# Local attention's sixteen steps written out, the second layer's weights brought in early, and two smaller moves at the head of a transformer kernel

## What is computed

```python
# block 1: 16-head causal attention, scores of masked keys set to 0 (not -inf), 64 wide heads
# block 2: mixture of 16 experts, top 2 of a softmax: y = x + sum_k w_k * (gelu(x @ W1[e_k] + b1) @ W2[e_k] + b2)
# block 3: counter = softplus(sum(relu(normed @ normed.T)) @ W1 + b1); concat([x, counter]) @ W2
# block 4: two layers of local attention, 8 heads, window 64
for l in range(2):
    h = shift_token(x)
    q, k, v = split(h @ wqkv[l])
    q = l2norm(q) * q_scale[l];  k = l2norm(k) * k_scale[l]
    q, k = rotary_xpos(q, k)                 # the same tables of cos, sin and scale for both layers
    x = x + local_attention(q, k, v) @ wo[l]
    h = layernorm(shift_token(x)) * ln_g[l] + ln_b[l]
    a, g = split(h @ w1[l] + b1[l])
    x = x + (a * gelu(g)) @ w2[l] + b2[l]
```

## Time and profile before

| | |
|---|---|
| time, 3 runs | 943.25 us median, 940.85 to 944.63 |
| profiled execution | 942.32 us; its span, first to last instruction, 940.5 us |
| busy PE, DVE, ACT, POOL | 786.5, 661.7, 590.3, 527.4 us |
| start, until the slots' staging begins | 0 to 19.3 us |
| block 1, 64 slots | to about 283 us |
| block 2, routing and experts | to about 440 us |
| block 3 | to about 496 us |
| block 4, local attention | to the end |

### The profile page before, as it was taken

One profiled execution on the slowest core, in us unless ns is written; L12 is line 12 of the kernel. 1 busy time (PEld: TensorE's weight loads), 2 busy tenths in 40 slices (PEclk: granted clock), 3 DMA queues, 4 the chain that ended last, 5 costly groups with the idle time before them and its releaser, 6 DMA issues. The chain is left out here.

```text
span 940.5 us, 21922 instructions
## 1 busy us (share of the span) xinstructions
PE 786.5 (84%) x6366; PEld 583.6 (62%) x6366; DVE 661.7 (70%) x1986; ACT 590.3 (63%) x1784; POOL 527.4 (56%) x603
## 2 busy tenths in 40 slices
PE   4899999999989844982554789999899999998884
PEld 3677777777769734981441356666666666666563
DVE  4777777777776765553675577888688888887555
ACT  2678888888860002761441568888788888886560
POOL 3644444444452773336834867777677777775411
PEclk9999999999999855995896899999999999999898
DMA  7544444444410081431100000000100000000001
GB/s 179 178 178 151 151 151 151 151 152 150 153 48 2 32 265 58 114 102 47 43 12 12 1 1 2 1 2 2 34 11 0 26 7 0 0 2 2 12 1 35
DMA packets 60796, 61.58 MB, mean 65 GB/s; under 512 B 13515, under 2 KB 48830, under 8 KB 60606
## 3 DMA queue, kind: packets, MB, share of 16 engines
q1 hardware_dynamic: 58686, 56.63, 18.4%
q0 software_dynamic: 2048, 4.20, 1.5%
HBM read 17.55 MB, written 23.00 MB: 43 GB/s over the span
## 5 line engine op out<-in xcount | busy, mean ns | idle before, releaser
L666 POOL TENSOR_TENSOR scratch<-scratch 128x256 f32<-128x256 f32 (+1 forms) x128 | 105.8, 827 | 132.6 <-DVE scratch L1644 132.6
L1043 ACT ACTIVATE scratch<-psum,scratch 128x128 f32<-128x128 f32 x256 | 113.9, 458 | 48.0 <-DVE scratch L1991 46.2
L794 POOL TENSOR_TENSOR big<-big 128x512 f32<-128x512 f32 x64 | 81.2, 1269 | 71.8 <-DVE big L1972 71.8
L898 ACT ACTIVATE scratch<-psum,scratch 128x256 f32<-128x256 f32 x256 | 118.0, 480 | 4.0 <-DVE scratch L1662 3.2
L803 POOL TENSOR_TENSOR scratch<-scratch,mhalf 128x16 f32<-128x16 f32 x32 | 93.0, 2906 | 16.8 <-DVE scratch L1978 16.8
L1415 PE MATMUL psum<-wqkv,scratch 128*128 128x512 f32 x128 | 71.2, 644 | 8.0 <-SPq L570 3.7
L1963 DVE TENSOR_REDUCE scratch<-big 128x8 f32<-128x512 f32 x64 | 43.7, 683 | 45.3 <-ACT big L1017 45.1
L1148 PE MATMUL psum<-scratch 128*128 128x256 f32 x240 | 61.8, 380 | 0.0
L1655 DVE TENSOR_TENSOR psum<-psum,causal 128x512 f32<-128x512 f32 x64 | 44.8, 700 | 23.0 <-PE psum L1171 22.9
L1989 DVE TENSOR_REDUCE scratch<-psum 128x4 f32<-128x512 f32 x64 | 44.0, 687 | 21.8 <-PE psum L1473 20.7
L1171 PE MATMUL psum<-scratch 64*128 64x128 f32 (+1 forms) x512 | 59.3, 350 | 0.0
(11 more groups left out here) (278 smaller groups left out, 2206.6 us busy)
## 6 DMA issues: line engine op xcount, KB each, us to landing
routed_in<-zfill SPq DMA_DIRECT2D x64, 256.0 KB, 2.2
scratch<-w_qkv SPq DMA_DIRECT2D x60, 193.0 KB, 2.2
scratch<-xT SPq DMA_DIRECT2D x60, 128.0 KB, 2.1
scratch<-routed_in SPq DMA_DIRECT2D x47, 64.0 KB, 1.8
routed_out<-scratch SPq DMA_DIRECT2D x23, 128.0 KB, 1.8
big<-in_L_ffn_W SPq DMA_DIRECT2D x1, 2048.0 KB, 8.9
wqkv<-in_L_ffn_wqkv SPq DMA_DIRECT2D x2, 512.0 KB
big<-in_L_ffn_b SPq DMA_DIRECT2D x1, 1024.0 KB, 11.8
```

The costliest lines, as they stand in the source:

```text
L666: pool.tensor_tensor(y, y, rs[s][:, t, :].unsqueeze(2).to_broadcast([P, 2, n]), ALU.mult).then_inc(b_p, 1)
L794: pool.tensor_tensor(qk[s][t][:, j * INNER:(j + 1) * INNER], t1[i % 2], t2[i % 2], ALU.add).then_inc(f_add, 1)
L898: last = act.activation(pr[s][:, t, h, :], scores_of(s)[:, h, t * S:(t + 1) * S], ACT.Exp, bias=nb[s][:, 2 * t + h:2 * t + h + 1], accum_o ...
L1043: last = act.activation(p1[k][:, h, t, :], bank(h)[:, t * P:(t + 1) * P], ACT.Exp, bias=nb1[k][:, h, t:t + 1], scale=rq8[s][:, t, 2 * a + ...
```

## The change

- Local attention's steps -3 to 17 are all written out; `run_steps` has no loop.
- The second layer's weights go to tiles of their own, cut from `w_qkv0` and `w_o0`, which are free after block 1's output projection. SyncE loads them (seven DMAs, 1.5 MB) right behind the experts' weights, and waits for their landing there, ahead of its wait for the routing. The five semaphores are raised for all 16 units at once.
- `lv` and `rotc` are gone: the engines read `vec` and `rot` at the layer's place. The two copies before step 0 and the loads during steps 6 to 10 are gone, with SyncE's waits for them.
- VectorE's slot begins with `z_out(g - 1)` and `inverse_sums(g + 1, 1 - s, 0)`, where the slot before ended with `z_out(g)` and `inverse_sums(g + 2, s, 0)`: VectorE's instructions keep their order, and the border between two passes of the loop falls elsewhere.
- x is loaded in four DMAs of 256 KB with a semaphore each, and VectorE's statistics wait for one chunk at a time.
- GpSimd raises `const_ready` after the first constants, and puts the four powers between the making of the others.

```diff
-            full = (4, UNITS - 4)
-            for n in range(-3, full[0]):
+            for n in range(-3, UNITS + 2):
                 step(n, n % 2)
-            with eng.Fori(0, (full[1] - full[0]) // 2) as i:
-                for s in range(2):
-                    step(i * 2 + (full[0] + s), s)
-            for n in range(full[1], UNITS + 2):
-                step(n, n % 2)
-                if after:
-                    after(n - full[1])
+                if after and n >= UNITS - 4:
+                    after(n - UNITS + 4)
...
+        spare = w_qkv0[:, :, :].rearrange("p a n -> p (a n)")
+        wqkv1s = (wqkv1[:, :], spare[:, 0:3 * INNER])
+        wo1s = (wo1[:, :, :], spare[:, 3 * INNER:3 * INNER + PAIRS1 * D].rearrange("p (a d) -> p a d", d=D))
+        wf1s = (wf1[:, :], spare[:, 3 * INNER + PAIRS1 * D:3 * INNER + PAIRS1 * D + 2 * HID])
+        wf2s = (wf2[:, :, :], w_o0[:, 0:3, :])
+        def lvec(m):
+            return vec[:, R_LV + LV * (m // B):R_LV + LV * (m // B + 1)]
...
-            sp_.dma_start(x0[:], A["L0_attn_resid_pre"].rearrange("b (t p) d -> p (b t) d", p=P)).then_inc(x_in, 16)
+            x_tiles = A["L0_attn_resid_pre"].rearrange("b (t p) d -> p (b t) d", p=P)
+            for c in range(NC):
+                sp_.dma_start(x0[:, c * CH:(c + 1) * CH, :], x_tiles[:, c * CH:(c + 1) * CH, :]).then_inc(x_in[c], 16)
...
             sp_.dma_start(w2all[:, :, KE, :], ...).then_inc(d_w, 16)
+            def second(dst, src_):
+                sp_.dma_start(dst, src_).then_inc(layer_in, 16)
+            layer1_load(second, 1, ("qk", "v", "o", "f1", "f2"))
+            sp_.wait_ge(layer_in, 7 * 16)
+            for ready in (f_wqk, f_wv, f_wwo, f_wf1, f_wf2):
+                sp_.sem_inc(ready, UNITS)
             sp_.wait_ge(d_route, MAPPED)
...
-            sp_.wait_ge(phase_done, 8)
-            sp_.dma_start(lv[:], vec[:, R_LV:R_LV + LV]).then_inc(layer_in, 16)
-            sp_.dma_start(rotc[:], rot[:, 0]).then_inc(layer_in, 16)
-            sp_.wait_ge(layer_in, 32)
-            (all of the piecewise loads of layer 1, down to the output)
...
+            def row_rstd(c):
+                pool.wait_ge(rows_var, c + 1)
+                pool.tensor_tensor(rstd[:, c, :], ve[:, c, :], mhalf[:, 0:CH], ALU.pow).then_inc(rows_rstd, 1)
+            (ident, causal; then memsets)
+            pool.drain().then_inc(const_ready, 1)
+            row_rstd(0)
+            (selects) ... row_rstd(1) ... row_rstd(2) ... row_rstd(3) ...
+            pool.drain().then_inc(const_ready, 1)
...
-                pe.matmul(qk_bank(m, i), hT[s][:, t * P:(t + 1) * P], wqkv1[:, j * INNER:(j + 1) * INNER],
+                pe.matmul(qk_bank(m, i), hT[s][:, t * P:(t + 1) * P], wqkv1s[m // B][:, j * INNER:(j + 1) * INNER],
...
-            dve.wait_ge(x_in, 16)
             for c in range(NC + 1):
                 if c < NC:
+                    dve.wait_ge(x_in[c], 16)
                     ln_stats(lambda t: x0[:, c * CH + t, :], CH, c, rows_var)
...
             def slot(g, r, q):
                 s = r % 2
+                if slot_live(g - 1): z_out(g - 1)
+                if slot_live(g + 1): inverse_sums(g + 1, 1 - s, 0)
                 if slot_live(g): probs_out(g)
...
                 if slot_live(g + 3): mask_scores(g + 3, 1 - s)
-                if slot_live(g): z_out(g)
-                if slot_live(g + 2): inverse_sums(g + 2, s, 0)
...
-                ca = rotc[:, 2 * j, t, :].unsqueeze(1).to_broadcast([P, H1, DH])
+                ca = rot[:, m // B, 2 * j, t, :].unsqueeze(1).to_broadcast([P, H1, DH])
```

More of the change, by code:

```diff
@@ L147, in build_program @@
         rstd = sb("rstd", [P, 4, CH])
-        x_in = sem("x_in")
+        x_in = [sem(f"x_in{c}") for c in range(NC)]
         w_in = sem("w_in")
@@ L614, in _ @@
                                pattern=[[-1, P]], channel_multiplier=1)
+            pool.memset(band[:], 0.0)
+            pool.memset(shift[:], 0.0)
+            pool.memset(carry[:], 0.0)
+            pool.memset(batch_rows[:], 1.0)
+            pool.memset(lower[:], 1.0)
+            pool.memset(ones[:], 1.0)
+            pool.drain().then_inc(const_ready, 1)
+            row_rstd(0)
             pool.affine_select(out=band[:], in_=band[:], compare_op=ALU.is_ge, fill=NEG, base=0,
                                pattern=[[0, TB], [-1, P]], channel_multiplier=1)
+            pool.affine_select(out=batch_rows[:], in_=batch_rows[:], compare_op=ALU.is_ge, fill=0.0, base=0,
+                               pattern=[[-H0, B]], channel_multiplier=1)
             pool.affine_select(out=shift[:], in_=shift[:], compare_op=ALU.not_equal, fill=1.0, base=1,
                                pattern=[[-1, P]], channel_multiplier=1)
+            pool.drain()
+            row_rstd(1)
+            pool.affine_select(out=band[:], in_=band[:], compare_op=ALU.is_ge, fill=NEG, base=WIN,
+                               pattern=[[0, TB], [1, P]], channel_multiplier=-1)
+            pool.affine_select(out=batch_rows[:], in_=batch_rows[:], compare_op=ALU.is_ge, fill=0.0, base=H0 - 1,
+                               pattern=[[H0, B]], channel_multiplier=-1)
             pool.affine_select(out=carry[:], in_=carry[:], compare_op=ALU.not_equal, fill=1.0,
@@ L622, in _ @@
             pool.drain()
-            pool.affine_select(out=band[:], in_=band[:], compare_op=ALU.is_ge, fill=NEG, base=WIN,
-                               pattern=[[0, TB], [1, P]], channel_multiplier=-1)
-            pool.drain()
+            row_rstd(2)
             pool.memset(band[0:WIN, 1, WIN:P], 0.0)
-            pool.drain()
-            pool.affine_select(out=band[0:WIN, 1, WIN:P], in_=band[0:WIN, 1, WIN:P], compare_op=ALU.is_ge, fill=NEG,
-                               base=0, pattern=[[1, WIN]], channel_multiplier=-1)
+            pool.affine_select(out=lower[:], in_=lower[:], compare_op=ALU.is_ge, fill=0.0, base=-1,
+                               pattern=[[1, P]], channel_multiplier=-1)
             pool.tensor_copy(identb[:], ident[:])
[L631 to L637, removed]
             pool.iota(ebase[:], [[EROWS, NE]], base=0, channel_multiplier=0, allow_small_or_imprecise_dtypes=True)
@@ L641, in _ @@
             pool.drain()
-            pool.affine_select(out=lower[:], in_=lower[:], compare_op=ALU.is_ge, fill=0.0, base=-1,
-                               pattern=[[1, P]], channel_multiplier=-1)
+            row_rstd(3)
+            pool.affine_select(out=band[0:WIN, 1, WIN:P], in_=band[0:WIN, 1, WIN:P], compare_op=ALU.is_ge, fill=NEG,
+                               base=0, pattern=[[1, WIN]], channel_multiplier=-1)
             pool.drain().then_inc(const_ready, 1)
-            for c in range(NC):
-                pool.wait_ge(rows_var, c + 1)
-                pool.tensor_tensor(rstd[:, c, :], ve[:, c, :], mhalf[:, 0:CH], ALU.pow).then_inc(rows_rstd, 1)
             pool.wait_ge(bo_ready, 1)
```

31 lines of the change are left out of this document (13 added, 18 removed).

## The result

The changed kernel takes 932.14 us (median of 4 runs, 931.32 to 935.10), the kernel before 943.77 (4 runs, 940.85 to 944.63): ratio 0.9892, 95% interval 0.9868 to 0.9916. On another chip the same pair gave 935.07 (6 runs) against 942.99 (20 runs), ratio 0.9915 [0.9889, 0.9940]. So by the medians the change saves 11.6 us on one chip and 7.9 on the other; 9.5 was forecast, and 933.8 us. The profiled execution took 935.1 us, its span is 933.2 (before: 942.32 and 940.5). It is the longest of its four, so its own difference of 7.3 us is smaller than that of the medians.

The account below looks back on a forecast made before the run. In local attention a step was taken to cost TensorE's work plus its waits. Start -2.4, borders -3.6, change of layer -4.0 and early load +0.5 make -9.5 us, from 943.25 to 933.8; range 926 to 938.5.

Parts of the forecast that it names:

- Change of layer, -4.0: Local attention: TensorE's 3.73 us wait for q and k weights goes; 4.0 us gained, 5.1 without the collision.
- the collision: Local attention: VectorE's product, just behind GpSimd's line, takes 1.26 us, not 0.16; forecast to persist; rival that it ends: 923.3, 10%.
- Start, -2.4: Kernel start: x in four chunks lets VectorE's statistics begin earlier; 2.4 us gained, bounds 0 and 3.9.
- Slots' border, -3.6: Block 1's slots: VectorE's pass border moved behind the mask is nearly hidden; 3.6 us gained, bounds 1.3 and 3.9.
- Early load, +0.5: Before the experts: SyncE's wait for the second layer's weights costs 0.5 us, bounds 0 and 12.8.
- Writing out the loop, 0: Local attention: the loop's border hides behind queued work, so writing it out gains 0 us, at most 4 x 0.1.
- The rival by which it gains: Local attention: each of four passes costs 0.58 us, so writing out the loop saves 2.3 us: 931.5; 4%.
- Copies before step 0, 0: Before local attention's step 0: the two removed copies were hidden, 0 us, at most 1.03.
- Slack: Local attention steps: VectorE, ScalarE and GpSimd were said to have 4 us and more to spare.
- the border's cost only moves: Block 1's slots: line 1638's lateness passes to line 1650, 1.3 us instead of 3.6; with start under 1, 937.5; 10%.
- the early load holds up the experts: SyncE's wait for the second layer's weights delays the experts, landing at 368.9: 948.6 us in all; 3%.
- nothing beyond the change of layer: Whole kernel: start and borders are covered elsewhere, so only the change of layer gains: 939.7; 5%.

Follow-up runs that it names:

- e9_only_layers: The changed kernel with one DMA for x, GpSimd's old order of constants and VectorE's old border; 939.49 us, ratio 0.9957 to the kernel before.
- e2_old_border: The changed kernel with VectorE's old border, in front of the copy of the probabilities; 935.16 us, ratio 0.9923 to the kernel before.
- e1_unrolled_only: The kernel before with only local attention's loop written out; 945.39 us, ratio 1.0013 to the kernel before.
- e6_pool_memset: The changed kernel with one unused 128x128 memset on GpSimd in each local attention step, before add_rot; 925.22 us, ratio 0.9800 to the kernel before.
- e7_late_load: The changed kernel with the second layer's seven loads, their wait and the semaphores moved behind SyncE's fetch loop; 933.69 us (1 run), before 943.27.

## Why the prediction was right, and where its steps were off

- **Change of layer, -4.0:** right, by the size too. -3.98 to -3.99 in both profiles of the changed kernel, -4.1 in the medians of e9_only_layers. The reckoning that the collision comes back in that step, and takes 1.1 of the 5.1 us, held.
- **Start, -2.4:** the mechanism was right, the size not. It is 3.7 us over the eleven profiles, near the upper bound of 3.9; the one pair of before and after shows 3.1 at the staging and 2.4 at the first slot, since that profile of the kernel before has the earliest start of the four with the old one. The term that failed is the 1.7 us by which three more issues were to push the small rows back: TensorE had them at 7.33 to 7.95 us with the new start, at 8.18 to 8.73 with the old. The other term, 2.2 us for the first chunk's landing, was read from another transfer (`zfill` to `routed_in`); the chunk needed 2.7 to 3.1.
- **Slots' border, -3.6:** the mechanism was right, the size not. The term that failed is "a border takes 0.42 us in all". Behind the mask it takes 0.61; 0.12 us of every pass is left, and the gain is 2.4 us (against e2_old_border). Against the kernel before it is 2.7, of which 0.2 is one long slot of the first pass there. Why it is longer behind the mask than behind the reciprocal no run tells. The sign named for it, under 0.1 us of more idle time before the moved copy, was missed with 0.36, and the copies at the border are 3.97 us apart, not 3.84. The bounds of 1.3 to 3.9 held.
- **Early load, +0.5:** too dear by a little; 0 to 0.4, 0.2 on the mean. The landing at about 348.2 agrees with a full queue that goes on at its speed: it was forecast 4.8 us behind the last expert weights, and those landed at 343.2 here.
- **Writing out the loop, 0:** right; by e1_unrolled_only it costs 0.2 us over six steps. The rival by which it gains has fallen. Copies before step 0, 0: nothing to see; the 1.03 us in front of the first projection is there as before.
- **The collision:** that it would persist was right. The reason given, that GpSimd gains on VectorE until they meet, was wrong but for one step: from step 2 to step 3 it comes 0.12 us nearer in both (0.09 us behind to 0.03 ahead before, 0.25 to 0.13 behind in e6_pool_memset). After that the distance keeps still at 0.12 to 0.13 us for ten steps in e6_pool_memset, and in the changed kernel at 0.01 to 0.03. The pipeline settles at a distance and keeps it; a shift of GpSimd by 0.14 us decides on which side. What moves VectorE's product from 0.09 us ahead in step 2 to just behind in step 3 no run tells.
- **The sum, -9.5:** by the measured parts it is -4.0 - 3.7 - 2.4 + 0.2 = -9.9 us, less what the moved border may give back in the experts; the two chips gave -11.6 and -7.9. That it came out so near is partly luck: the start was taken 1.3 us too small and the border 1.2 too large. The spread between executions is as large as any single part.
- **Slack:** "4 us and more to spare" is not what the earlier trace rows show of ScalarE, which has 3.2 us in the step of 22.82. Nothing in the sum hangs on it.

The other rivals: "the border's cost only moves" is true of 0.12 of 0.27 us; "the early load holds up the experts" has fallen with the distances under e7_late_load, and "nothing beyond the change of layer" with e9_only_layers: 4.1 us by itself, where the whole change gives 7.9 to 11.6.

## What to carry to other kernels

Where two engines' instructions start within 0.1 us of one another and one of them is eight times as long in some steps, read both timelines and try the other order before anything larger: a memset of 0.2 us gave 9 us here, more than the resident weights, the start and the borders singly. Try the border of a hardware loop on each engine at the place where that engine waits longest in every slot (of the three places tried here, in front of a wait of 0.36 us it was hidden, in front of one of 0.25, behind the mask, it was not); where it lies behind queued work, writing the loop out gains nothing. Judge parts of 1 to 3 us by the distance between two instructions of the trace that enclose them, in several executions of each kernel, and not by single runs that lie 7 us apart: one pair of profiles made the start 2.4 us where eleven make it 3.7. And take such a distance apart where two waits can end it.

## What the runs showed of the hardware

- A loop border costs VectorE 0.41 us behind a reciprocal, 0.61 behind the mask, nothing that can be seen in front of a wait of 0.36 us or of queued work; behind the reciprocal the first one costs more (0.72 idle in the earlier trace rows, and 0.72 in e2_old_border).
- Four issues of 256 KB hold SyncE's queue for 2.09 us, and the statistics that wait for the first start 2.7 to 3.1 us after its issue; the small rows behind them came no later for it.
- A product of VectorE with two inputs in SBUF takes 0.16 to 0.17 us when it starts 0.09 to 0.25 us ahead of GpSimd's 128x512 product, and 1.25 to 1.27 us, to the other's end, when it starts 0.01 to 0.03 us behind it.
- The same code from the last expert output to step 1 takes near 132.3 us in some profiles and near 133.8 in others, with TensorE's granted clock rising and falling at other places between its two levels; this hides gains of 1 to 2 us in single executions.
